# Which operand of a two-branch graph layer is loaded first, and how many of its opening products are whole float32

## The reference, cut to what matters

```python
h = jnp.maximum(_layernorm(x, axis=-1), 0.0)      # x: 4096 x 128, eps 1e-5
out1 = _cxin_conv(h,  adj, eps1, W1, b1)          # adj: 4096 x 4096, float32
out2 = _cxin_conv(x2, adj, eps2, W2, b2)
# _cxin_conv(x, a, ...): ax = a @ x; h = ax + (1 + eps) * ax
#                        3 times: h = relu(h @ W[i].T + b[i])
x = x + jnp.concatenate((out1, out2), axis=1) @ Wm.T + bm
```

## Time and profile before

| | |
|---|---|
| time, median of 3 runs | 406.74 us (406.16 to 407.13) |
| the profiled execution | 406.39 us |
| its span, first to last instruction | 404.7 us |
| TensorE busy | 400.2 us (99%) |
| VectorE, ScalarE busy | 219.1 us, 219.4 us (54% each) |
| GpSimd busy | 30.5 us (8%) |
| moved by DMA | 76.21 MB, 188 GB/s over the span |

### The profile page before, as it was taken

The page is one execution under the profiler, slowest core; times in us unless marked ns, Lnnn a source line. Parts: engine busy times, 40 slices in busy tenths (PEclk is TensorE's granted clock), DMA queues, the critical chain, the costliest instruction groups (busy, mean ns, idle before and its releaser), DMA issues.

```text
span 404.7 us, 4822 instructions
## 1 busy us (share of the span) xinstructions
PE 400.2 (99%) x1751; PEld 325.4 (80%) x1751; DVE 219.1 (54%) x258; ACT 219.4 (54%) x259; POOL 30.5 (8%) x35
## 2 busy tenths in 40 slices
PE   8999999999999999999999999999999999999997
PEld 2788888888888888888888888888888888888886
DVE  3998887656464434551645517345373444755223
ACT  4877667657564533555433556334565335766034
POOL 0243332100010000000100001000000000000100
DMA  7997786754636165334574336653175550740100
GB/s 303 420 377 285 296 314 238 244 208 160 232 146 210 44 241 205 109 120 191 186 280 164 122 128 236 230 206 141 67 262 204 207 196 38 275 166 2 52 0 28
DMA packets 14029, 76.21 MB, mean 188 GB/s; under 512 B 1920, under 2 KB 2176, under 8 KB 6080
## 3 DMA queue, kind: packets, MB, share of 16 engines
q1 hardware_dynamic: 12240, 71.18, 46.9%
q0 software_dynamic: 1200, 3.93, 2.9%
q10 hardware_dynamic: 576, 0.92, 0.6%
HBM read 73.93 MB, written 2.10 MB: 188 GB/s over the span
## 4 chain that ended last, share of the span: by engine, by line
PE 97%; DMA 2%; ACTq 0%; DVE 0%; issue 0%; DVEq 0%
PE acc L591 24%; PE acc L588 24%; PE acc L587 24%; PE second_acc L587 3%; PE second_acc L591 3%; PE second_acc L588 3%; PE hidden L588 3%; PE hidden L591 3%; PE hidden L587 3%; PE acc L605 2%; PE second_acc L605 2%; DMA adj_raw<-adj_first 2%; PE second_acc L619 1%; PE merged L588 1%; PE merged L591 1%; PE merged L587 1%
## 5 line engine op out<-in xcount | busy, mean ns | idle before, releaser
L588 PE MATMUL acc<-adj_hi,feat_hi 128*128 128x512 f32 x432 | 168.1, 389 | 0.0
L587 PE MATMUL acc<-adj_hi,feat_lo 128*128 128x512 f32 x432 | 168.1, 389 | 0.0
L591 PE MATMUL acc<-adj_lo,feat_hi 128*128 128x512 f32 x432 | 168.0, 389 | 0.0
L447 DVE TENSOR_TENSOR adj_lo<-adj_raw,adj_hi 128x2048 fp32r<-128x2048 f32 x48 | 108.3, 2289 | 36.7 <-ACT adj_hi L277 35.8
L277 ACT ACTIVATE adj_hi<-adj_raw 128x2048 fp32r<-128x2048 f32 x48 | 90.3, 1925 | 16.5 <-PE acc L591 14.6
L453 DVE TENSOR_TENSOR act_lo<-act_f,act_hi 128x512 fp32r<-128x512 f32 x60 | 41.0, 690 | 105.3 <-ACT act_f L297 105.3
L588 PEld LDWEIGHTS acc<-adj_hi,feat_hi 128*128 128x128 f32 x432 | 81.1, 188 | 17.1
L587 PEld LDWEIGHTS acc<-adj_hi,feat_lo 128*128 128x128 f32 x432 | 81.1, 188 | 17.1
L591 PEld LDWEIGHTS acc<-adj_lo,feat_hi 128*128 128x128 f32 x432 | 81.1, 188 | 16.8
L296 ACT ACTIVATE act_hi<-hidden,bias 128x512 fp32r<-128x512 f32 x45 | 30.9, 687 | 96.2 <-PE hidden L591 96.2
L507 DVE TENSOR_TENSOR adj_lo<-adj_raw,adj_hi 128x2048 fp32r<-128x2048 f32 x14 | 31.5, 2289 | 6.5 <-ACT adj_hi L315 6.2
(11 more groups left out here) (91 smaller groups left out, 251.3 us busy)
## 6 DMA issues: line engine op xcount, KB each, us to landing
adj_raw<-adj_tiles SPq DMA_DIRECT2D x62, 1024.0 KB, 5.1
x_rows<-x_tiles SPq DMA_DIRECT2D x15, 256.0 KB, 7.1
x_res<-x_t POOLq DMA_DIRECT2D x8, 256.0 KB, 6.4
out_t<-y_sb POOLq DMA_DIRECT2D x7, 256.0 KB, 2.3
adj_raw<-adj_second SPq DMA_DIRECT2D x2, 512.0 KB, 6.6
adj_raw<-adj_first ACTq DMA_DIRECT2D x2, 256.0 KB, 5.0
adj_raw<-adj_first SPq DMA_DIRECT2D x2, 256.0 KB, 4.7
w_raw<-w_t SPq DMA_DIRECT2D x1, 512.0 KB, 5.8
```

Of the source, the lines that this page charges most:

```text
L447: nc.vector.tensor_tensor(adj_lo[:, u % RING, :], adj_raw[:, u % RING, :], f32(adj_hi[:, u % RING, :]), ALU.subtract).then_inc(lo_made, 1)
L587: nc.tensor.matmul(out, lhs_lo, rhs_hi, start=start, stop=False)
L588: nc.tensor.matmul(out, lhs_hi, rhs_hi, start=False, stop=False)
L591: return nc.tensor.matmul(out, lhs_hi, rhs_lo, start=False, stop=stop)
```

## The change

It alters the opening only, and the vector steps of every unit of x.

- Loads: x goes out first on SyncE's queue and x2 second; quarter 1 moves to ScalarE's queue, in the place of x.
- TensorE: 12 warm-up products in place of 8. The float32 products cover the first unit and the first half of the second (6 blocks). The second half of the second unit is multiplied with x2 in three passes a block, at the end of `opening_of_second`. The x branch is done unit by unit (`opening_of_first`, `opening_of_second`) in place of half by half over both.
- ScalarE: the x2 features of unit 0 are split early, the halves of `adj` pieces and of x in another order, and unit 2 is copied in one piece.
- VectorE: the statistics of x come ahead of all remainders. Epsilon is the bias of ScalarE's square root (a constant tile `ln_eps`), and is folded into the Newton step, in place of an add of its own. The Newton step still has three instructions.
- GpSimd: one wait on the scale of unit 0 at its start; then for every unit x2's remainder, then x's.

```diff
--- before
+++ after
@@ constants @@
-    SECOND_UNIT = len(PIECES[0]) - 1
     X_SLOTS = 4
-    WARM_UP = 8
+    WARM_UP = 12
...
@@ SyncE @@
             def load_x2(u):
                 if u >= X_SLOTS:
-                    sp.wait_ge(feat2_lo_made, x2_count(u - X_SLOTS))
+                    sp.wait_ge(feat2_lo_made, u + 1 - X_SLOTS)
                 sp.dma_start(x2_rows[:, u % X_SLOTS], x2_tiles[u]).then_inc(x2_loaded[u % X_SLOTS], 16)
+            load_x(0)
             load_x2(0)
-            for s, i in ((0, 1), (0, 2), (1, 0), (1, 1)):
+            for s, i in ((0, 2), (1, 0), (1, 1)):
@@ GpSimd @@
-            low_of_x(0)
-            for u in range(1, U):
+            pool.wait_ge(rstd_made, 1)
+            for u in range(U):
                 low_of_x2(u)
                 low_of_x(u)
-                if u == 1:
-                    low_of_x2(0)
@@ ScalarE @@
             def std_of_x(u):
                 act.wait_ge(var_made, u + 1)
-                nc.scalar.activation(std[:, :], var_eps[:, :], ACT.Sqrt).then_inc(std_made, 1)
+                nc.scalar.activation(std[:, :], mean_var[:, :, 1], ACT.Sqrt, bias=ln_eps[:, :]).then_inc(std_made, 1)
-            def high_of_half(s, h):
...
-            for i in (0, 3):
-                if i == 3:
-                    act.dma_start(x_rows[:, 0], x_tiles[0]).then_inc(x_loaded[0], 16)
+            for i in (0, 1, 3):
                 to, piece_of, done = piece_load(0, i)
                 act.dma_start(to, piece_of).then_inc(done, 16)
-            act.wait_ge(zero_made, 1)
+            act.wait_ge(constants_made, 2)
             nc.scalar.activation(root_of_zero[:, :], zero[:, :], ACT.Sqrt)
-            for i in range(len(PIECES[0]) - 1):
-                piece_high(0, i)
+            piece_high(0, 0)
             std_of_x(0)
-            piece_high(0, len(PIECES[0]) - 1)
-            piece_high(1, 0)
+            piece_high(0, 1)
+            high_of_x2(0)
             act.wait_ge(rstd_made, 1)
             rectify_half(0, half_relu_made, half_feat1_made)
+            piece_high(0, 2)
+            piece_high(0, 3)
+            rectify_half(1, relu_made, feat1_hi_made)
+            piece_high(1, 0)
             piece_high(1, 1)
-            rectify_half(1, relu_made, feat1_hi_made)
             high_of_x2(1)
-            high_of_half(2, 0)
             std_of_x(1)
-            high_of_half(2, 1)
+            high_of_opening(2)
             high_of_opening(3)
             rectify(1)
-            high_of_x2(0)
@@ VectorE @@
                 for j in range(JB):
                     last = nc.vector.bn_aggr(mean_var[:, j, :], stats[:, j, :])
-                step(last)
-                nc.vector.tensor_scalar(var_eps[:, :], mean_var[:, :, 1], LN_EPS, None, ALU.add).then_inc(var_made, 1)
+                last.then_inc(var_made, 1)
...
+                dve.wait_ge(var_made, u + 1)
                 dve.wait_ge(std_made, u + 1)
                 step(nc.vector.reciprocal(r0, std[:, :]))
-                step(nc.vector.tensor_tensor(nt, r0, r0, ALU.mult))
-                step(nc.vector.scalar_tensor_tensor(nt, nt, -0.5, var_eps[:, :], ALU.mult, ALU.mult))
+                step(nc.vector.scalar_tensor_tensor(nt, r0, -0.5, r0, ALU.mult, ALU.mult))
+                step(nc.vector.scalar_tensor_tensor(nt, mean_var[:, :, 1], LN_EPS, nt, ALU.add, ALU.mult))
...
-            nc.vector.memset(zero[:, :], 0.0).then_inc(zero_made, 1)
-            for i in range(2):
-                piece_low(0, i)
+            nc.vector.memset(zero[:, :], 0.0).then_inc(constants_made, 1)
+            nc.vector.memset(ln_eps[:, :], LN_EPS).then_inc(constants_made, 1)
             variances(0)
             scale_and_shift(0)
-            for i in range(2, len(PIECES[0])):
-                piece_low(0, i)
-            for i in range(len(PIECES[1])):
-                piece_low(1, i)
+            piece_low(0, 0)
+            piece_low(0, 1)
+            piece_low(0, 2)
+            piece_low(0, 3)
             variances(1)
+            piece_low(1, 0)
+            piece_low(1, 1)
             scale_and_shift(1)
@@ TensorE @@
-            def raw_aggregate(s):
+            def raw_aggregate(s, pieces):
...
-                for i in range(len(PIECES[s])):
+                for i in pieces:
...
-            def norm_aggregate():
...
+            def opening_of_first():
+                out = opening_bank(0, late)
+                pe.wait_ge(half_feat1_made, 1)
+                pe.wait_ge(fine_hi_made, HALF)
+                passes(out, 0, late, [(feat_hi, adj_hi)], range(HALF), start=True)
+                pe.wait_ge(fine_lo_made, HALF)
+                passes(out, 0, late, [(feat_hi, adj_lo)], range(HALF))
+                pe.wait_ge(feat1_hi_made, 1)
+                pe.wait_ge(hi_made, 1)
+                passes(out, 0, late, [(feat_hi, adj_hi)], range(HALF, JB))
+                pe.wait_ge(lo_made, 1)
+                passes(out, 0, late, [(feat_hi, adj_lo)], range(HALF, JB))
                 pe.wait_ge(feat1_lo_made, 1)
+                signal(0, late, passes(out, 0, late, [(feat_lo, adj_hi)]))
+
+            def opening_of_second():
+                halves = range(HALF), range(HALF, JB)
+                out = opening_bank(1, late)
+                pe.wait_ge(fine_hi_made, len(PIECES[0]))
+                passes(out, 1, late, [(feat_hi, adj_hi)], halves[0], start=True)
+                pe.wait_ge(fine_lo_made, len(PIECES[0]))
+                passes(out, 1, late, [(feat_hi, adj_lo)], halves[0])
+                pe.wait_ge(hi_made, 2)
+                passes(out, 1, late, [(feat_hi, adj_hi)], halves[1])
+                passes(out, 1, late, [(feat_lo, adj_hi)])
+                pe.wait_ge(lo_made, 2)
+                passes(out, 1, late, [(feat_hi, adj_lo)], halves[1])
+                pe.wait_ge(feat2_hi_made, 1)
+                pe.wait_ge(feat2_lo_made, 1)
+                signal(0, late, passes(opening_bank(1, first), 1, first,
+                                       [(feat_hi, adj_hi), (feat_lo, adj_hi), (feat_hi, adj_lo)], halves[1]))
...
-            for at in range(len(PIECES)):
-                raw_aggregate(at)
-            norm_aggregate()
+            raw_aggregate(0, range(len(PIECES[0])))
+            raw_aggregate(1, [0])
+            opening_of_first()
+            opening_of_second()
```

More of the change, by code:

```diff
@@ L92, in gnn_layer_kernel @@
         mean_var = sb("mean_var", [P, JB, 2])
-        var_eps = sb("var_eps", [P, JB])
         std = sb("std", [P, JB])
@@ L106, in gnn_layer_kernel @@
         zero = sb("zero", [P, 1])
+        ln_eps = sb("ln_eps", [P, 1])
         act_f = sb("act_f", [P, 2, CW])
@@ L134, in gnn_layer_kernel @@
         fine_lo_made = sem("fine_lo_made")
-        zero_made = sem("zero_made")
+        constants_made = sem("constants_made")
         unit_used = sem("unit_used")
@@ L177, in piece_load @@
             return adj_raw[:, s, cols], (adj_first, adj_second)[s][i], raw_loaded[s] if n is None else fine_loaded[n]
-        def x2_count(u):
-            return {0: 2, 1: 1}.get(u, u + 1)
         def quarter(q):
@@ L244, in low_of_x2 @@
                 pool.wait_ge(x2_loaded[u % X_SLOTS], 16 * (u // X_SLOTS + 1))
-                pool.wait_ge(feat2_hi_made, x2_count(u))
+                pool.wait_ge(feat2_hi_made, u + 1)
                 nc.gpsimd.tensor_tensor(feat_lo[:, 1, rows, :], x2_rows[:, u % X_SLOTS], f32(feat_hi[:, 1, rows, :]),
@@ L598, in opening_bank, with passes @@
                 return (second_acc if c else acc)[b]
-            def passes(out, s, b, passes_of, start=False):
+            def passes(out, s, b, passes_of, blocks=range(JB), start=False):
                 u = OPENING[s][0]
                 for k, (feat, adj) in enumerate(passes_of):
-                    for j in range(JB):
+                    for j in blocks:
                         slot, cols = columns(s, j)
                         last = nc.tensor.matmul(out[:, :], feat[:, b, u * JB + j, :], adj[:, slot, cols],
-                                                start=start and k == 0 and j == 0, stop=False)
+                                                start=start and k == 0 and j == blocks[0], stop=False)
                 return last
-            def raw_aggregate(s):
+            def raw_aggregate(s, pieces):
                 u, c = OPENING[s]
@@ L621, in raw_aggregate @@
                 last.then_inc(raw_used, 1)
-            def norm_aggregate():
[L625 to L639, removed]
-                pe.wait_ge(feat1_lo_made, 1)
-                for s in range(2):
-                    signal(0, late, passes(opening_bank(s, late), s, late, [(feat_lo, adj_hi)]))
@@ L649, in passes_aggregate @@
                 if b == first:
-                    pe.wait_ge(feat2_hi_made, x2_count(u))
+                    pe.wait_ge(feat2_hi_made, u + 1)
                     passes(out, s, b, [(feat_hi, adj_hi)])
-                    pe.wait_ge(feat2_lo_made, x2_count(u))
+                    pe.wait_ge(feat2_lo_made, u + 1)
```

## The result

The changed kernel takes 407.48 us (median of 20 runs, 406.82 to 408.87), the one before 406.29 (20 runs, 406.06 to 407.13). The ratio is 1.0027, 95% interval 1.0020 to 1.0034: 1.19 us slower. I had forecast 406.5, which is some 0.2 less than the 406.74 of the kernel before in its first three runs, and called it no change. So the sign is wrong. That 407.48 lies inside my range of 405.8 to 407.6 is luck: the range was made from the terms of the opening, on a median of three runs that lay 0.45 too high, and nearly all of the loss is elsewhere. Three executions of later batches (one of e5, two of the kernel before) took 679 to 1500 us and are left out of all medians and ratios.

A forecast was written before the change was run, and what follows sets the result against it. TensorE, busy 400.2 of 404.7 us, was taken to bound the kernel. The terms -0.36 + 0.22 + 0.05 + 0.10 - 0.20 = -0.19 on a median of 406.74 gave about 406.5 us, range 405.8 to 407.6.

The forecast's parts named there:

- All else is priced at nothing: Everything outside the opening and the vector steps of x: 0, as TensorE does the same products in the same order.
- Products: Second unit on TensorE: two blocks move from float32 products to three short passes each, -0.36 us.
- Late start: First unit: x2 lands at 5.85 instead of 4.5, so the unit ends at 9.49 instead of 9.27, +0.22 us.
- Warm-up: TensorE's start: four more warm-up products, mostly hidden under the wait for x2, +0.05 us, ends 0 and 0.25.
- Chain of x: Vector and scalar steps of x in the opening: scale ready at 7.3 instead of 9.9, over 1 us to spare.
- The tight spot: Remainder of the second unit's last half: TensorE may wait if Pool's step goes between, +0.10 us, ends 0 and 0.35.
- The stall: TensorE's wait near 20.05 us for unit 2's late remainder goes away, -0.20 us, ends -0.20 and 0.
- Queues: Loads behind the opening: slot 1's load and two behind it are issued later, the delay is absorbed, 0.
- A: TensorE's wait for x2 in the opening: x2 comes late, at 7.0, giving 407.7 us; chance 0.15.
- B: Opening's gains are hidden: warm-up costs 0.25, Pool's lock 0.35, the stall returns by 0.20, giving 407.2 us; chance 0.15.

The follow-up runs named there:

- e5: Kernel before with unused 32-byte tiles ahead of `adj_hi` and behind `adj_lo`: 415.91 us, ratio 1.0233.
- e1: Changed kernel with `ln_eps` declared where `var_eps` was, so the layers' weights lie at their old offsets: 406.21 us against 406.32, ratio 1.0001.
- e2: Kernel before with the declaration of `var_eps` moved behind `zero`, so the layers' weights lie 32 bytes lower: 407.62 us, ratio 1.0031.
- e3: e1 with 8 warm-up products instead of 12: 406.15 us, ratio 1.0007, runs in two heaps (405.8 to 406.2 and 407.6 to 408.0).
- e12: Kernel before with the epsilon edit alone, `ln_eps` declared in the place of `var_eps`: 406.15 us against 406.44, ratio 0.9996.
- e10: Kernel before with 64 unused bytes ahead of `feat_hi` and 64 behind `feat_lo`: 416.10 us, ratio 1.0237.
- e6: Kernel before with 32 unused bytes ahead of `feat_hi` and 32 behind `feat_lo`: 416.07 us, ratio 1.0240.
- e9: Kernel before with 32 unused bytes ahead of `adj_hi` and 32 behind `feat_lo`: 406.65 us, ratio 1.0004.
- e11: Kernel before with 64 unused bytes ahead of `w_raw` and 96 ahead of `act_f`: 405.86 us, ratio 0.9985.

## Why the prediction was wrong, step by step

- **"All else is priced at nothing, because TensorE does the same products in the same order."** This step failed. The products behind the opening are the same, but their operands' places aren't, and that costs 1.16 of the 1.2 us: the stretch goes from 354.85 to 356.01, e1 takes it away and e2 brings it alone. The removed and added tiles stood in the full diff, and I read them as arithmetic only.
- **Products, -0.36.** The chain has -0.34.
- **Late start, +0.22.** The landing of x2 was right (5.65 for 5.85). But with the warm-up's part the late start came to +0.67, not +0.27, and this alone turns the opening's -0.19 into a small loss.
- **Warm-up, +0.05, ends 0 and 0.25.** This term was mis-sized. The warm-up held TensorE to 6.10, 0.15 past my start and within my ends. But I bounded only its length. That the first product behind it still ran at 1.2 GHz (0.83 us where I had 0.53, fresh start included: +0.30) was outside my ends, because I took the clock after eight products in one execution for a fact of the kernel.
- **Chain of x.** The scale was ready at 6.9 (forecast 7.3), because x was there at 4.2. The chain itself was longer than I had it, 2.69 us for 2.51: the square root with the bias tile takes 0.30 where it took 0.21. TensorE waited on none of it, so the cover held.
- **The tight spot, +0.10.** GpSimd (Pool) did go between VectorE's two remainders, as these rows of VectorE's and GpSimd's timelines show (two steps of 1.2 us take 3.42):

```profile
12.90 3.42 DVE L483 TENSOR_TENSOR adj_lo<-adj_raw,adj_hi 128x1024 fp32r<-128x1024 f32 x2
```

```profile
13.27 1.97 POOL L242 TENSOR_TENSOR feat_lo<-x_rows,feat_hi 128x512 fp32r<-128x512 f32 x1 [1.20 <-ACT feat_hi L314]
```

They ended at 16.3, as worked out (16.4). But TensorE was 0.44 later than forecast and wanted them only at 16.69, so the term was 0. That was luck of the late start. In e3, which starts at 5.51, TensorE's weight loads do wait there until 16.19, and its eighteen passes of the second unit take 4.38 us in place of 4.08:

```profile
PEld second_acc L590 <- DVE adj_lo L483: 0.4, 1, 0.4
```

So the mechanism stands, at 0.3 us, inside my ends. The new Newton step still takes 0.58 us beside GpSimd, at 23.45, as I had said.
- **The stall, -0.20.** Right (-0.23 from unit 2 on), and e12 shows which edit does it.
- **Queues, 0.** Right: no wait on a load behind the opening.
- **Rivals.** A (407.7) and B (407.2) come near the measured time for the wrong reasons. For A, x2 was on time. Of B's costs only the warm-up's was paid. Without the layout the change comes out as in e1, 406.21 against 406.32 of the kernel before: the forecast's "no change" would have held. It would have held in part by offsets, as the start cost more than forecast and the tight spot less.

## What to carry to other kernels

When a change adds, drops or reorders tiles, list where every TensorE operand lies before and after. Give each product's weights and moving operand like start offsets; alike modulo 256 bytes is what these runs show to be fast, and alike modulo 64 is not enough (e10). Compare two traces first by the time of the same instructions in the untouched stretch: a difference that grows there in small steps (0.04 us here) isn't a wait, and no view of waits shows it. A start that rests on TensorE's clock having risen is read from several runs, not from one profile.

## What was unexpected of the hardware

- Start offsets of weights and moving operand unlike modulo 128 bytes: 233.3 ns a pass instead of 226.7 for 512 columns, 9.6 to 9.7 us over the kernel (e5, e6, e10). Alike at 0 or at 32: 226.7 (e9).
- The whole float32 products don't show this: with x2 at 64 and `adj_raw` at 0 (e5, e6, e9) they are 0.43 us apart, as with both at 0.
- Products of unlike offsets also slow passes of alike offsets behind them, for 2 to 10 instructions. With like pairs in both sets (e11) two slow ones are left at each change of set.
- The first product behind 5.1 us of back-to-back warm-up was still at 1.2 GHz (0.83 us), while the granted clock showed 1.00.
